# Four graph layers with layer norms on one core: the third layer's matrix in one-scale form, and a reordered start

## The reference

```
L0: y = (A x + x) W0 + b0;  x1 = LN(x + y / max(|y|, 1e-12))
L1: S = exp(8 tanh((x1 q)(x1 k)^T / sqrt(128) / 8)) * A;  x2 = LN(x1 + (S / rowsum S) x1 v)
L2: x3 = LN(x2 + (gate terms with relation A) x2 W2 + b2)
L3: dis = deg^-1/2 (deg = row sums of A); L = I - dis A dis; T2 = 2 L L - I
    out = LN(x3 + relu(x3 W[0] + L x3 W[1] + T2 x3 W[2] + b3))
```

## Time and profile before

| | us |
|---|---|
| median of 3 runs | 728.53 (728.14 to 728.96) |
| the profiled execution, its own time | 728.63 |
| its span, first to last instruction | 726.5 |
| PE busy | 645.3 (89%) |
| DVE busy | 616.1 (85%) |
| ACT busy | 383.5 (53%) |
| POOL busy | 72.3 (10%) |
| mean granted TensorE clock | 0.967 of 2.4 GHz |

### The profile page before, as it was taken

The page is one execution under the profiler, slowest core; times in us unless marked ns, Lnnn a source line. Parts: engine busy times, 40 slices in busy tenths (PEclk is TensorE's granted clock), DMA queues, the critical chain, the costliest instruction groups (busy, mean ns, idle before and its releaser), DMA issues. The chain is left out here.

```text
span 726.5 us, 17484 instructions
## 1 busy us (share of the span) xinstructions
PE 645.3 (89%) x7478; PEld 488.2 (67%) x7478; DVE 616.1 (85%) x1562; ACT 383.5 (53%) x525; POOL 72.3 (10%) x49
## 2 busy tenths in 40 slices
PE   4937955889999999999999999999999999869894
PEld 3533633456886688667866687668866786638894
DVE  3789898998999899898989899989989897879525
ACT  3928914782359244944467255924494447613402
POOL 0020001000200111002200120011100220020002
PEclk9978996999999999999999999999999999989998
DMA  7100001000100020000200020002000010000102
GB/s 263 45 29 1 1 1 30 0 2 1 31 3 1 2 60 2 1 3 1 60 1 2 1 60 2 1 2 60 2 1 2 5 27 2 1 1 2 31 2 59
DMA packets 20013, 14.54 MB, mean 20 GB/s; under 512 B 864, under 2 KB 18912, under 8 KB 19936
## 3 DMA queue, kind: packets, MB, share of 16 engines
q1 hardware_dynamic: 18816, 12.91, 5.8%
q10 hardware_dynamic: 1120, 0.52, 0.3%
HBM read 9.24 MB, written 4.19 MB: 18 GB/s over the span
## 5 line engine op out<-in xcount | busy, mean ns | idle before, releaser
L240 POOL TENSOR_TENSOR small<-small,minus_half 128x8 f32<-128x8 f32 x39 | 67.9, 1745 | 602.7 <-DVE small L528 479.5
L1215 PE MATMUL av<-vhi,p_hi 128*128 128x129 f16 x512 | 90.1, 221 | 8.8 <-DVE p_lo L776 8.5
L375 ACT ACTIVATE att<-r,coef 128x1024 f32<-128x1024 f32 x64 | 70.4, 1100 | 49.8 <-PE r L1102 49.2
L1218 PE MATMUL av<-vhs,p_lo 128*128 128x129 f16 x512 | 89.9, 220 | 0.0
L1217 PE MATMUL av<-vlo,p_hi 128*128 128x128 f16 x512 | 89.8, 219 | 0.0
L771 DVE TENSOR_TENSOR att<-att,adjT 128x1024 f32<-128x1024 f32 x64 | 78.1, 1221 | 10.9 <-ACT att L377 10.9
L776 DVE SCALAR_TENSOR_TENSOR p_lo<-p_hi,att 128x1024 f16<-128x1024 f16 x64 | 78.1, 1221 | 0.0
L1100 PE MATMUL r<-gr,lap 128*128 128x128 f16 x448 | 75.8, 219 | 0.0
L1102 PE MATMUL r<-gr,lap 128*128 128x128 f16 x448 | 75.8, 219 | 0.0
L1101 PE MATMUL r<-gr,lap 128*128 128x128 f16 x448 | 75.8, 219 | 0.0
L1102 PE MATMUL r<-xq,lap 128*128 128x128 f16 x448 | 75.4, 219 | 0.0
(11 more groups left out here) (300 smaller groups left out, 1924.6 us busy)
## 6 DMA issues: line engine op xcount, KB each, us to landing
x<-in_x SPq DMA_DIRECT2D x8, 512.0 KB, 4.3
lap<-in_adj SPq DMA_DIRECT2D x8, 512.0 KB, 9.4
out<-outb SPq DMA_DIRECT2D x7, 512.0 KB, 3.4
out<-att SPq DMA_DIRECT2D x1, 384.0 KB, 2.8
b_bc<-in_L_gnn_bias SPq DMA_DIRECT2D x3, 64.0 KB, 7.2
x<-in_L_gnn_weight ACTq DMA_DIRECT2D x1, 192.0 KB, 8.1
out<-att SPq DMA_DIRECT2D x1, 128.0 KB, 2.7
x<-in_L_gnn_q ACTq DMA_DIRECT2D x1, 64.0 KB, 3.5
```

What stands on the lines that cost most here:

```text
L240: return nc.gpsimd.tensor_tensor(dst, src, minus_half[:], ALU.pow)
L375: nc.scalar.activation(att[:, s], (r1, r0)[t % 2][:], ACT.Tanh, scale=c_tanh).then_inc(S["th"], 1)
L1215: mm(acc, p_hi[:, s, chunk(j)], vhi[:, t, 0:D + 1], start=(t == 0 and j % 3 == 0), stop=False, skip_group_check=True)
L1218: l_ = mm(acc, p_lo[:, s, chunk(j)], vhs[:, t, 0:D + 1], start=False, stop=(t == C - 1), skip_group_check=True)
```

## The change

The third layer works on rows scaled by the root of the degree. With M = -A diag(1/deg) the scaled rows z = sqrt(deg) x give sqrt(deg) L x = (I + M) z, so that the three weights are recombined (W0 + W1 + W2; W1 + 4 W2; W2) and the matrix has one scale by column: `lap_s` in place of two factors and the diagonal. Norm 2 multiplies its argument by dis squared, norm 3 adds EPS times deg, the bias becomes `b3_rows`. `ln_arg` is rewritten. `lap_row`, its diagonal tiles, the matmuls that spread dis and the copy of them are gone; ACT makes `lap` hi straight from adjT (blocks 0 and 1 in the head, 2 to 7 and the bias rows after y0 in iteration 0), DVE makes lo (0 and 1 in iteration 0, 2 to 7 in iteration 1). SP issues the broadcasts behind the adjacency. The x0 product is made by chunks of 128 columns, each as soon as its a_lo is there; half 0 is projected before the last chunk; DVE takes the adjT pass of chunks 0 and 1, and a_lo of chunk 7 straight from the transposes. The weights are prepared in pieces. In iteration -1 DVE's `y_half(0)` now stands ahead of `y0_half(1)` (in iteration 0 too), `weights_split(1, 2)` stands where the diagonal tiles were made, `lap_scales` where dis was copied. POOL takes the norm's root ahead of dis.

```diff
-LAP_UP = 64.0
+LAP_UP = 256.0
...
-LN_ARG = 5
-LN_LINKS = 6
+LN_ARG = (4, 4, 5, 4)
+LN_LINKS = (5, 5, 6, 5)
+DVE_COPIES = 2
...
-                if c == 1:
-                    for dst, src in ((b0_bc[:], b0), (b2_bc[:], b2), (b3_bc[:], b3.rearrange("a b d -> (a b d)")),
-                                     (wj_bc[:], gw[0:D]), (wi_bc[:], gw[D:2 * D]),
-                                     (wr_gb[:, 0:1], gw[2 * D:2 * D + 1]), (wr_gb[:, 1:2], gb)):
-                        sp.dma_start(dst, src.partition_broadcast(P)).then_inc(S["w_in"], 16)
+            for dst, src in ((b0_bc[:], b0), (b2_bc[:], b2), (b3_bc[:], b3.rearrange("a b d -> (a b d)")),
+                             (wj_bc[:], gw[0:D]), (wi_bc[:], gw[D:2 * D]),
+                             (wr_gb[:, 0:1], gw[2 * D:2 * D + 1]), (wr_gb[:, 1:2], gb)):
+                sp.dma_start(dst, src.partition_broadcast(P)).then_inc(S["bc_in"], 16)
...
+                if nxt:
+                    pool.wait_ge(S["e0_c"], 8 * (i + 2))
+                    inverse_root(small[:, 4, ROOT], small[:, 4, ARG]).then_inc(S["norm_r"], 1)
                 if is_first(i, -1):
                     pool.wait_ge(S["deg_ok"], C)
                     inverse_root(dis[:], deg[:]).then_inc(S["dis_ok"], 1)
-                if nxt:
-                    pool.wait_ge(S["e0_c"], 8 * (i + 2))
-                    inverse_root(small[:, 4, ROOT], small[:, 4, ARG]).then_inc(S["norm_r"], 1)
...
-                copy(adjT[:, :, chunk(c)], src, LO_UP * P_UP).then_inc(S["adj_cp"], 1)
+                if c == C - 1:
+                    act.wait_ge(S["adj_lo"], C)
+                if c >= DVE_COPIES:
+                    copy(adjT[:, :, chunk(c)], src, LO_UP * P_UP).then_inc(S["adj_cp"], 1)
+                if c == C - 3:
+                    act.wait_ge(S["y0_mm"], 1)
+                    copy(yT[:, 0, half(0)], r1[:, half(0)], Y0_DOWN).then_inc(S["y0_hi"], 1)
...
             def lap_hi_part(*rows):
+                act.wait_ge(S["lap_sc"], 1)
                 for c in rows:
-                    act.wait_ge(S["lap_st"], 2 * (c + 1))
-                    copy(lap[:, 0, c, :], (lap_f, lap_g)[c % 2]).then_inc(S["lap_hi"], 1)
+                    copy(lap[:, 0, c, :], adjT[:, c, :], lap_s[:, c:c + 1]).then_inc(S["lap_hi"], 1)
+
+            def bias_rows():
+
+                act.wait_ge(S["bc_in"], 16 * 7)
+                for c in range(C):
+                    l_ = copy(b3_rows[:, c], b3_bc[:], root_deg[:, c:c + 1])
+                l_.then_inc(S["b3_ok"], 1)
...
-                if is_first(i, -1):
-                    degrees(0, 5)
                 if nxt:
                     y0_half(1)
                 if is_first(i, -1):
-                    degrees(5, C)
+                    degrees(0, C)
+                    lap_hi_part(0, 1)
+                if is_first(i, 0):
+                    lap_hi_part(2, 3, 4, 5, 6, 7)
+                    bias_rows()
                 if prev:
...
-                tt(sm[:, 0], me, mo, ALU.add)
-                tt(sm[:, 1], me, mo, ALU.subtract)
-                ch.link(tt(sm[:, 2], st[:, :, 0, 2], st[:, :, 1, 2], ALU.add))
-                tt(sm[:, 3], sm[:, 1], sm[:, 1], ALU.mult)
-                ch.link(ts(sm[:, 4], sm[:, 0], -0.5, None, ALU.mult))
-
-                ch.link(stt(sm[:, 0], sm[:, 3], D / 4.0, sm[:, 2], ALU.mult, ALU.add))
-                ch.mark(ts(sm[:, ARG], sm[:, 0], 1.0 / D, EPS, ALU.mult, ALU.add))
+                tt(sm[:, 0], me, mo, ALU.subtract)
+                ch.mark(stt(sm[:, 2], st[:, :, 0, 2], 0.0 if k_ == 3 else D * EPS, st[:, :, 1, 2], ALU.add, ALU.add))
+                stt(sm[:, 4], me, -1.0, mo, ALU.mult, ALU.subtract)
+                ch.wait()
+                if k_ == 3:
+                    stt(sm[:, 1], sm[:, 0], 0.25, sm[:, 0], ALU.mult, ALU.mult)
+                    ch.link(stt(sm[:, 3], sm[:, 2], 1.0 / D, eps_deg[:, cs], ALU.mult, ALU.add))
+                    ch.mark(tt(sm[:, ARG], sm[:, 3], sm[:, 1], ALU.add))
+                else:
+                    ch.link(stt(sm[:, 1], sm[:, 0], 0.25, sm[:, 0], ALU.mult, ALU.mult))
+                    if k_ == 2:
+                        ch.link(stt(sm[:, 3], sm[:, 2], 1.0 / D, sm[:, 1], ALU.mult, ALU.add))
+                        ch.mark(tt(sm[:, ARG], sm[:, 3], dis2[:, cs], ALU.mult))
+                    else:
+                        ch.mark(stt(sm[:, ARG], sm[:, 2], 1.0 / D, sm[:, 1], ALU.mult, ALU.add))
                 ch.end()
+
+            def shift(sm):
+
+                return stt(sm[:, SHIFT], sm[:, 4], 0.5, sm[:, ROOT], ALU.mult, ALU.mult)
...
             def weights_max():
-                dve.wait_ge(S["w_in"], 16 * 11)
-                tt(w3c[:, 2], w3_sb[:, 0], w3_sb[:, 2], ALU.subtract)
+                dve.wait_ge(S["w_in"], 16 * 4)
+                tt(w3c[:, 2], w3_sb[:, 0], w3_sb[:, 1], ALU.add)
                 nc.vector.tensor_copy(w3c[:, 0], w3_sb[:, 2])
-                nc.vector.tensor_copy(w3c[:, 1], w3_sb[:, 1]).then_inc(S["m_cp"], 1)
+                stt(w3c[:, 1], w3_sb[:, 2], 4.0, w3_sb[:, 1], ALU.mult, ALU.add).then_inc(S["m_cp"], 1)
                 dve.wait_ge(S["m_cp"], 2)
+                tt(w3c[:, 2], w3c[:, 2], w3_sb[:, 2], ALU.add).then_inc(S["m_cp"], 1)
+                dve.wait_ge(S["m_cp"], 3)
                 for j, w in enumerate((w0_sb, m_sb, v_sb, w2_sb[:], w3c.rearrange("p k d -> p (k d)"))):
...
+            def weights_scale():
+                dve.wait_ge(S["w_sum"], 1)
+                w_ch.link(ts(wpow[:], m7[:, 3 * P:3 * P + 5], MIN_MAX, None, ALU.max))
+                w_ch.link(ts(wpow[:].bitcast(U32), wpow[:].bitcast(U32), POW2_MASK, None, ALU.bitwise_and))
+                w_ch.link(nc.vector.reciprocal(winv[:], wpow[:]))
+                w_ch.link(ts(winv[:], winv[:], SUM_UP, None, ALU.mult))
...
+            def weights_split(*which):
+
+                parts = ((w0_sb, w0s[:, 0], w0s[:, 1]), (m_sb, ms[:, 0], ms[:, 1]),
+                         (v_sb, vs[:, 0], vs[:, 1]), (w2_sb[:], w2s[:, 0], w2s[:, 1]),
+                         (w3c, w3s[:, :, 0], w3s[:, :, 1]))
+                for j in which:
+                    w, hi, lo = parts[j]
+                    w_ch.link(ts(hi, w, winv[:, j:j + 1], None, ALU.mult))
+                    w_ch.mark(stt(lo, w, winv[:, j:j + 1], hi, ALU.mult, ALU.subtract))
+            def gate_weights():
...
+            dve.wait_ge(S["ident_ok"], 3)
+            ts(ident_up[:], ident[:], ADJ_UP, None, ALU.mult).then_inc(S["iu_ok"], 1)
             for c in range(C):
+                src = cd((r0[:], r2)[c % 2])
+                if c < DVE_COPIES:
+                    dve.wait_ge(S["adj_hi"], c + 1)
+                    ts(adjT[:, :, chunk(c)], src, LO_UP * P_UP, None, ALU.mult).then_inc(S["adj_cv"], 1)
+                    dve.wait_ge(S["adj_cv"], c + 1)
+                if c == C - 1:
+                    dve.wait_ge(S["adj_hi"], C)
+                    l_ = stt(a_lo[:, :, chunk(c)], src, ADJ_UP, a_hi[:, :, chunk(c)], ALU.mult, ALU.subtract)
+                else:
+                    if c >= DVE_COPIES:
+                        dve.wait_ge(S["adj_cp"], c + 1 - DVE_COPIES)
+                    l_ = stt(a_lo[:, :, chunk(c)], adjT[:, :, chunk(c)], ADJ_UP / (LO_UP * P_UP), a_hi[:, :, chunk(c)],
+                             ALU.mult, ALU.subtract)
+                l_.then_inc(S["adj_lo"], 1)
+                if c == 1:
                     weights_max()
+                if c == 3:
+                    weights_scale()
+                    weights_split(0)
+                if c == 5:
+                    dve.wait_ge(S["y0_hi"], 1)
+                    stt(yT[:, 1, half(0)], r1[:, half(0)], Y0_DOWN, yT[:, 0, half(0)], ALU.mult, ALU.subtract).then_inc(S["y0_lo"], 1)
+
+            def lap_scales():
+
+                dve.wait_ge(S["dis_ok"], 1)
+                tt(dis2[:], dis[:], dis[:], ALU.mult)
+                stt(lap_s[:], dis[:], -LAP_UP / (LO_UP * P_UP), dis[:], ALU.mult, ALU.mult)
+                ts(eps_deg[:], deg[:], EPS, None, ALU.mult)
+                tt(root_deg[:], deg[:], dis[:], ALU.mult).then_inc(S["lap_sc"], 1)
...
-                    tt(lap[:, 1, c, :], (lap_f, lap_g)[c % 2], lap[:, 0, c, :], ALU.subtract).then_inc(S["lap_lo"], 1)
+                    stt(lap[:, 1, c, :], adjT[:, c, :], lap_s[:, c:c + 1], lap[:, 0, c, :],
+                        ALU.mult, ALU.subtract).then_inc(S["lap_lo"], 1)
...
-                stt(z.u[:], cd(r2), c_u, row(b3_bc[:]), ALU.mult, ALU.add).then_inc(S["u_ok"], 1)
+                stt(z.u[:], cd(r2), c_u, b3_rows[:], ALU.mult, ALU.add).then_inc(S["u_ok"], 1)
...
-                        if is_first(i, 1):
-                            if t in (1, 3, 6):
-                                lap_row({1: 5, 3: 6, 6: 7}[t])
-                            if t in (2, 5, 7):
-                                lap_lo_part({2: 5, 5: 6, 7: 7}[t])
+                        if is_first(i, 1) and t != 4:
+                            lap_lo_part(t + 1 if t < 4 else t)
```

(75 more changed lines are left out.)

131 lines of the change are left out of this document (37 added, 94 removed).

## The result

The changed kernel takes **725.38 us** (median of 8 runs, 723.14 to 727.27) where the one before took 728.68 (728.14 to 729.55) beside it: a ratio of 0.9957, 95% interval 0.9941 to 0.9973. It is faster by 3.3 us, 7.9 had been forecast, and it lies 0.4 us outside the range. Its profiled execution took 725.35 us, with a span of 723.2.

A forecast was written before the change was run, and what follows sets the result against it. PE was taken to bound the middle iterations. Terms 2.0 + 0.37 + 0.75 + 0.37 + 0.8 + 2.2 + 1.4 = 7.9 us, off 728.6, gave 720.7 us; the range was 716.5 to 725.0.

The forecast's parts named there:

- iterations 1 to 6: Middle iterations: norm 0's shorter small operations cut PE's wait from 1.0 to 0.6 us, saving 6 x 0.37 = 2.2 us.
- Head: Start to first layer's second half: chunk loop of 5.8 us per two chunks, y_half(1) at 39.1 against 41.10, 2.0 us saved.
- Rival B: The head gives nothing: slower chunk loop, or x1 stage pays up to 1.3 us for clock; 722.7 to 725, chance 0.2.
- Iteration 0: First mask 0.45 us earlier without lap_row(2), 0.3 less wait for y0: 0.75 us, bounds 0 and 1.6; norm 0 adds 0.37.
- Iteration 1: DVE bounds; three lap_row and lap_lo pairs become six lap_lo, shortening PE's p_lo waits: 0.8 us, bounds 0.4 and 1.1.
- Tail: After the middle: norm 1's 0.37, norms 3 and 2 (0.29 + 0.17), last norm's arguments 0.58; sum 1.4 us.
- The broadcasts: Head: issued last on SP's queue, they let adjacency chunks land earlier than PE can use them, and cost nothing.
- The matmuls of 128 columns: x0 product: 192 matmuls start 0.056 us apart, loads overlapping; by the skill page's 81 ns, 4.8 us more, some 725.5.
- rival F: x0 product: weight loads bind the short matmuls, 0.10 instead of 0.056 us each, 8.4 us on the loop: 729; chance 0.02.
- C: The clock falls well: shorter slow stretches in the first iterations, or iteration 0 gives its upper bound: 716.5 to 719; chance 0.12.
- D: Slower: PE stays at 1.2 GHz through the whole chunk loop, waiting in every turn: 732; chance 0.05.
- E: Transfers bound nothing after chunk 2, the rest was hidden: head and iteration 0 zero, norms partly: 726 to 728; chance 0.06.

The follow-up runs named there:

- mended kernel: The changed kernel with first-half statistics put back ahead of y0's second low half in iterations 1 to 6, as before the change: 720.10 us, ratio 0.989.

## Why the prediction was wrong

**The step that failed** is the one for iterations 1 to 6, "6 x 0.37 = **2.2 us**. What is late next is still that wait." It took from these iterations only what the norm's operations save, and left out that `y0_half(1)` now stands ahead of the first half's statistics in them too. The description of the change speaks of this order for the first two iterations alone, and the working for none. The 0.87 us of statistics had filled the wait between x1's first half and ACT's copy (0.21 us of it were left before); behind the low half they hold up `xq` instead, for which PE waits. Nothing in the earlier trace rows shows a wait for `xq`, since there was none: it had to be found by following on DVE what each moved instruction fills now and whom it delays. The price, 0.85 us six times, is 5.1 of the 7.9 us, and the mended kernel's 720.1 is 0.6 from the forecast of 720.7. That nearness is in part luck. In the mended kernel's profile (719.09 us) the five stretches of the table gave 4.0, 2.3, 0.5, 1.9 and 0.9 us where 2.4, 1.1, 0.8, 1.9 and 1.8 were forecast: only the equal periods are right term by term. The range missed the changed kernel's time because no rival had a new wait in the middle, and by no more than 0.4 us because the first two stretches gave 1.3 more than forecast.

**Head.** The loop of 5.80 us for two chunks, bound by a_lo, came exactly so; its start was mis-sized. Product 0 ran at the full clock in that profile (1.45, not 2.8), transposes 2 in 1.04, not 1.6, and x came 0.4 us earlier; `y_half(1)` started at 36.94 instead of 39.1. So the term was 4.2, not 2.0, and outside its own bounds of 1.0 to 2.5. The upper bound was summed wrong: by its own terms the full clock from 13.7 on saves 1.35 in product 0 and 0.56 in the transposes, which makes 3.9. (Another slip: 19.5 and three loops of 5.8 are 36.9, not 36.7.) In three other profiled runs of related kernels product 0 took 2.3 to 2.7 us or the transposes behind it were slow, and the second half's projection started at 37.6 to 38.1 instead of 36.06: the forecast had taken the worse of two values that both occur.

**Rival B** came true in its size, 1.3 us between transposes and scores, but not as the fixed price of the missing diagonal matmuls: the mended kernel has none either and took 7.41. Without filler the stretch of the head is slow in three of four profiles without those matmuls and in none of five with them, so they may help; that stays open.

**Iteration 0** gave 1.6 against 1.12, by other parts than forecast. The wait before the first attend fell from 2.66 to 2.19, as worked out, but PE's wait for y0 grew from 1.09 to 1.64 where it was to lose 0.3: up to there only 0.28 came of the 0.75. From there to x1's transposes 0.90 came instead of the norm's 0.37, and 0.42 from the x1 stage (8.37 against 8.79), which no term had. With the old order these parts are 1.10, 0.36 and 0.26: the order only moves time between the first two.

**Iteration 1** gave 0.3 less than nothing where 0.8 was forecast. The order took its 0.85 here too; without it 0.54 is left. That is what PE's three waits for p_lo lost: 3.0 us before, 2.5 now (0.97 to 0.64, 0.86 to 0.59, 1.18 to 1.24), where 0.8 had been worked out.

**Tail:** 1.26 us with one norm 0 in it, where 1.77 was forecast. The rest is the clock's, by an estimate. PE waits 5.8 us (before) or 5.5 (after) for the low half of layer 2's rows of batch 6 and then runs slowly at first: in the 8 us behind that wait the granted clock was 0.74 before (644.22 to 652.22) and 0.68 after (641.45 to 649.45). (The page of before has this dip too, 8 tenths in the slice from 636 to 654 us, beside those in the first 130 us and one at the end.) It was 0.63 in the mended kernel and 0.78 in the changed kernel with the old order everywhere, whose code there is the same, and the stretch from the last root to the end took 148.1 and 147.0 us: 0.07 us for each 0.01. By that the kernel before would have been some 0.4 us longer at 0.68, and the tail gives 1.7.

**The broadcasts** were right as a cause and wrong as a term: alone they are worth 3.5 us, within the whole change nothing that can be told, since the new head hides most of the late chunk by itself. **The matmuls of 128 columns** start 0.056 us apart (26 in 1.45 us), each with its own weight load: rival F falls, and so does the estimate made from the Trainium skill, "TensorE: Matmul & The Clock Gate", section "Back-to-back issue gap" (about 81 ns): by it the chunk loop's 26 matmuls would have taken 2.1 us. Rivals C, D and E did not come about: no profile showed the chunk loop at half speed beyond its first turn, and the norms alone are worth 4.9.

## What to carry to other kernels

In a stream that executes in order, an instruction's place is worth as much as its length: work that fills a wait is free, and the same work behind the wait is paid in full by whoever stands after it. For every line of a diff that moves, ask in each iteration, not only where the change aims, which wait it filled and who is now behind it. And try each part of a change alone: here two small parts gave all of the gain that can be told, a third took most of it back, and the largest gave nothing that can be told.

## What was unexpected of the hardware

The granted clock of some stretches varies from run to run, in the same code. The changed kernel's runs spread over 4.1 us (723.14 to 727.27), those of the kernel before, in four sets, over 1.1 to 2.3, and those with only the broadcasts moved over 0.35 (724.84 to 725.19, four runs). In the profiles the differences sit where PE comes out of a wait: product 0 took 1.45 us, or 2.3 to 2.7; the x1 stage of the head 7.4 or 8.9; the 8 us behind the wait for batch 6's layer-2 rows had between 0.63 and 0.80 of the clock. It is not the head alone: in iteration 1 the stretch from 127.94 to 134.20 of the mended kernel had 0.73, and the same code in the changed kernel (129.53 to 135.76) 1.00. It cost nothing there: both profiles have the same 0.54 us beside the order's 0.85. Why one kernel spreads less than another these runs don't show.

Sixteen unread matmuls brought x1's transposes to the full clock in three of the four places where they stand alone. It was not the length of the idle time behind them: the fast ones had waited 1.77, 2.61 and 2.71 us, the slow ones 2.17. Nor are fast transposes enough: in five fast cases with filler the stretch to the scores took 6.37 once and 7.87 to 7.96 four times, for the matmuls behind the next wait of about 1 us were slow again; nine stretches in the table, with transposes of 1.97 us, took less, 7.33 to 7.76. And the record of the clock is coarse: in the profile with the broadcasts early it says 1.00 over product 0, whose matmuls start 0.107 us apart, against 0.056 in the changed kernel's.
